# Top-k attention: the left-over values of a row are kept for each half of its chunks apart

## The reference, cut to what matters

```
q, k, v = heads(conv1x1(x, Wq, bq)), heads(conv1x1(x, Wk, bk)), heads(conv1x1(x, Wv, bv))
scores = einsum('bhnd,bhmd->bhnm', q, k) * 32 ** -0.5      # 2 x 8 x 2304 rows of 2304
kth = top_k(scores, 64)[0][..., -1:]                       # the 64th largest of each row
attn = softmax(where(scores >= kth, scores, lowest))
o = einsum('bhnm,bhmd->bhnd', attn, v)
```

## Time and profile before

| | us |
|---|---|
| median of 3 runs | 5124.61 (5120.05 to 5127.47) |
| profiled execution | 5125.56 |
| its span | 5123.8 |
| mean granted TensorE clock, share of full speed | 0.832 |

### The profile page before, as it was taken

One profiled execution on the slowest core, in us unless ns is written; L12 is line 12 of the kernel. 1 busy time (PEld: TensorE's weight loads), 2 busy tenths in 40 slices (PEclk: granted clock), 3 DMA queues, 4 the chain that ended last, 5 costly groups with the idle time before them and its releaser, 6 DMA issues. The chain is left out here.

```text
span 5123.8 us, 106951 instructions
## 1 busy us (share of the span) xinstructions
PE 4131.7 (81%) x32161; PEld 2787.5 (54%) x32161; DVE 4325.4 (84%) x25276; ACT 4155.0 (81%) x6082; POOL 1502.6 (29%) x362
## 2 busy tenths in 40 slices
PE   8577677776777677767777767899899999999999
PEld 4354444444444444544454444443567777777776
DVE  4999999999999999999999999430368888888886
ACT  2799799998999789989999899644268888888885
POOL 0344445544454444444444444200100000000000
PEclk9677777777777777777777777899799999999999
DMA  6000000000000000000000000200330111111112
GB/s 214 7 18 17 8 17 17 8 17 15 11 17 17 7 17 8 18 16 8 18 18 8 17 17 8 67 6 0 133 93 25 34 25 34 25 34 32 27 34 94
DMA packets 79597, 154.62 MB, mean 30 GB/s; under 512 B 8120, under 2 KB 49464, under 8 KB 73528
## 3 DMA queue, kind: packets, MB, share of 16 engines
q1 hardware_dynamic: 78904, 146.72, 10.1%
HBM read 99.50 MB, written 47.19 MB: 29 GB/s over the span
## 5 line engine op out<-in xcount | busy, mean ns | idle before, releaser
L542 POOL TENSOR_TENSOR a_probs<-a_scores,a_probs 128x2304 f32<-128x2304 f32 x288 | 1460.7, 5093 | 1671.3 <-ACT a_probs L465 1671.3
L560 DVE MAX8 a_top<-a_scores 128x8 f32<-128x36 f32 x18432 | 1831.6, 180 | 57.4 <-ACT a_scores L449 45.9
L376 PE MATMUL a_ps_t<-ident,a_probs 128*128 128x128 f32 x5184 | 965.2, 323 | 594.4 <-ACT a_probs_t L460 458.0
L376 PEld LDWEIGHTS a_ps_t<-ident,a_probs 128*128 128x128 f32 x5184 | 665.8, 162 | 884.4 <-ACT a_probs_t L460 597.8
L465 ACT ACTIVATE a_probs<-a_scores,a_steep_kth 128x2304 f32<-128x2304 f32 x290 | 641.2, 2211 | 183.5 <-DVE a_minus_max L692 183.5
L1292 DVE TENSOR_SCALAR_CACHE_REDUCE b_soft<-b_ps_s 128x2304 f32<-128x2304 f32 x288 | 735.0, 2552 | 26.5 <-PE b_ps_s L1151 8.5
L460 ACT ACTIVATE a_probs_t<-a_ps_t 128x512 f32<-128x512 f32 (+1 forms) x1440 | 725.8, 545 | 18.4 <-PE a_ps_t L376 6.2
L1167 PE MATMUL b_ps_t<-ident,b_soft 128*128 128x128 f32 x5184 | 727.0, 276 | 1.6 <-DVE b_soft_t L1298 0.6
L1167 PEld LDWEIGHTS b_ps_t<-ident,b_soft 128*128 128x128 f32 x5184 | 578.5, 140 | 170.3 <-ACT b_soft_t L1256 60.1
L453 ACT ACTIVATE a_probs<-a_probs,a_minus_max 128x2304 f32<-128x2304 f32 x288 | 637.9, 2215 | 30.5 <-issue 18.5
L366 PE MATMUL a_ps_s<-a_k_stack,a_q_ring 128*128 128x512 f32 (+1 forms) x1465 | 647.3, 601 | 15.9 <-ACT a_scores L449 11.1
(11 more groups left out here) (133 smaller groups left out, 4138.6 us busy)
## 6 DMA issues: line engine op xcount, KB each, us to landing
a_k_stack<-k_parts SPq DMA_DIRECT2D x72, 288.0 KB, 6.0
b_k_stack<-k_parts SPq DMA_DIRECT2D x72, 288.0 KB, 6.0
a_q_ring<-q_parts SPq DMA_DIRECT2D x294, 64.0 KB
b_q_ring<-q_parts SPq DMA_DIRECT2D x294, 64.0 KB
k_parts<-p_high SPq DMA_DIRECT2D x36, 256.0 KB, 2.1
k_parts<-p_rest SPq DMA_DIRECT2D x36, 256.0 KB, 2.1
q_parts<-p_high SPq DMA_DIRECT2D x36, 256.0 KB, 2.0
q_parts<-p_rest SPq DMA_DIRECT2D x36, 256.0 KB, 2.0
```

The lines of the kernel that those rows point to most:

```text
L376: last = pe.transpose(ps_t[(NTG * s + g) % 2][:, P * m:P * m + P], probs[s % 2][:, P * (m0 + m):P * (m0 + m) + P], cst["ident"][:, :])
L542: pool.tensor_tensor(probs[u][:, :], scores_all[:, 2 * (p % 2) + u, :], probs[u][:, :], ALU.subtract).then_inc(masked_ready, 1)
L560: last = dve.max(top8[s // 2 % 2][:, s % 2, c, :], scores_all[:, s % 4, CHUNK * c:CHUNK * c + CHUNK])
```

## The change: what it does, and the diff

`prepare` now takes the eight largest of the fourth to eighth values for chunks 0 to 31 and for chunks 32 to 63 apart: four MAX8 over 160 values for a pair instead of two over 320. The first half's eight go to column 0 of the REST rows, the second half's to column 1. The candidates are read as before, 72 x 3 a row, and hold 8 more real values. A new operation `eighths` takes the larger of the two halves' eighth values. `beyond` is formed from it and from the chunks' eighths, and stands behind `place` now. The low value is set once, before the loop, in column 2 alone.

```diff
-        extremes, beyond = sb("extremes", [P, 2, 2]), sb("beyond", [P, 2])
+        extremes, eighths, beyond = sb("extremes", [P, 2, 2]), sb("eighths", [P, 2]), sb("beyond", [P, 2])
...
+            def rest_of_half(tops, u, half):
+                return dve.max(tops[:, u, CHUNKS:CHUNKS + REST, half],
+                               tops[:, u, CHUNKS // 2 * half:CHUNKS // 2 * (half + 1), KEEP:8])
+
             def prepare(pair, tops):
 
                 wait_alone(dve, tops_taken, 2 * pair + 1)
-                counted(dve.max(tops[:, 0, CHUNKS:CHUNKS + REST, 0], tops[:, 0, 0:CHUNKS, KEEP:8]))
+                counted(rest_of_half(tops, 0, 0))
+                counted(rest_of_half(tops, 0, 1))
                 wait_alone(dve, tops_taken, 2 * pair + 2)
-                counted(dve.max(tops[:, 1, CHUNKS:CHUNKS + REST, 0], tops[:, 1, 0:CHUNKS, KEEP:8]))
+                counted(rest_of_half(tops, 1, 0))
+                counted(rest_of_half(tops, 1, 1))
...
                 after(guesses)
                 written = [0, 0]
+                counted(dve.tensor_tensor(eighths[:, :], tops[:, :, CHUNKS + REST - 1, 0],
+                                          tops[:, :, CHUNKS + REST - 1, 1], ALU.max))
                 for u in range(2):
                     rows = counted(dve.tensor_scalar(below_of(u), candidates(u), guess[:, u:u + 1], None, ALU.is_ge,
                                                      ALU.add, accum_out=above_guess[:, u:u + 1]))
-                counted(dve.tensor_tensor(beyond[:, :], extremes[:, :, 1], tops[:, :, CHUNKS + REST - 1, 0], ALU.max))
                 after(rows)
...
                 counted(dve.tensor_scalar(place[:, :], above_guess[:, :], -1.0, TOPK - 1.0, ALU.mult, ALU.add))
+                counted(dve.tensor_tensor(beyond[:, :], extremes[:, :, 1], eighths[:, :], ALU.max))
...
-                dve.memset(top8[n][:, :, CHUNKS:CHUNKS + REST, 1:KEEP], LOWEST)
+                dve.memset(top8[n][:, :, CHUNKS:CHUNKS + REST, 2:KEEP], LOWEST)
```

## The result

| | before | after |
|---|---|---|
| median, us | 5124.6 | 5076.1 (5075.2 to 5080.4) |
| ratio, with its 95% interval | | 0.9908 (0.9894 to 0.9921) |
| profiled span, us | 5123.8 | 5073.4 |
| recounts of a tile / corrections | 19 / 2 | 13 / 2 |

What follows compares the result with a forecast made beforehand. A ring through ScalarE was taken to set the period, with VectorE having a little room and searches paid in full. 5125.6 - 47 for searches + 3.5 for uncovered work gave 5082, against the median 5081 us; range 5057 to 5117.

Steps and rivals of the forecast that it cites:

- Who sets the period: Top-k hand-over: the ring runs through ScalarE, whose copy of the count sets the threshold; an ordinary pair takes 20.52 us.
- the 0.87 us of the earlier trace: Hand-over: when VectorE is late, the threshold (L691) was said to follow ScalarE's copy (L470) after 0.87 us.
- Prepare, +0.12 us: Ahead of the next scores: four maxima over 160 cost 0.91 against 0.79 us, hidden in 0.25 us of room.
- the 23 us "by it": Alternative by the Trainium skill: all added durations count, 0.05 + 0.11 us a pair beyond the room, sum about 5101.
- Select, +0.15 us, with 0.20 of room: Ahead of the doubts: eighths and the moved beyond add 0.07 us each, together 0.15, hidden in the ordinary pair.
- Rival 1: The hand-over isn't hidden: added work shows in some 130 to 144 pairs, 5088 to 5101 us; chance 0.13.
- What a search costs: Top-k stage: nothing else gets done while VectorE searches, so each is paid in full, 6.96 us plain, 14.30 corrected.
- How many go: Rows in doubt fall from 13.5 to 9.4: 4.7 plain recounts and one of two corrections go, together -47 us.
- cause B: Doubt because the left-overs' eighth value reaches the 64th: 1.45 in 10000 rows, 0.22 with the halves apart.
- cause A: Doubt because the largest of the chunks' eighth values reaches the 64th: 2.4 in 10000 rows.
- Cost without cover, +3.5 us: 14 pairs with 0.08 us of room pay 1 us, 8 without room 2.2; with the last pair +3.5.
- Rival 3: Slower: three more instructions a pair shift VectorE's jumps, each stop 1.5 us, 29 more eat the gain; chance 0.07.

Runs made afterwards that it cites:

- e5: The changed kernel with four spare two-column tensor_scalar operations between the guess and the count, ahead of the doubts: 5112.5 us, 0.9977 of before.
- e12: The kernel before with one spare two-column tensor_scalar behind the eleventh chunk maximum of the second tile: 5334.7 us, 1.0407.
- e9: The changed kernel with 64 one-column memsets ahead of VectorE's loops, which shifts the code: 5076.9 us, 0.9910 of before.
- e10: The kernel before with 64 one-column memsets ahead of VectorE's loops, which shifts the code: 5122.0 us, 0.9996.
- e1: The kernel before with no row ever in doubt, so without its 19 recounts and 2 corrections: 4981.3 us, 0.9717.
- e2: The changed kernel with no row ever in doubt, so without searches: 4978.6 us, 0.9711 of before.
- e11: The kernel before with beyond behind place, a spare two-column tensor_scalar in select and two spare MAX8 behind the extremes, all recounts kept: 5120.4 us, 0.9989.
- e4: The changed kernel with a strict comparison, so a value equal to the 64th raises no doubt: 5080.8 us, 0.9910 of before.
- e3: The kernel before with beyond behind place and three spare two-column tensor_tensor, one in select and two behind the extremes, all recounts kept: 5171.3 us, 1.0086.
- e7: The kernel before with beyond behind place and three spare two-column operations of one source (tensor_scalar), one in select, two behind the extremes: 5169.9 us, 1.0085.
- e6: The changed kernel with four spare two-column tensor_scalar operations behind the extremes, ahead of the next scores: 5151.0 us, 1.0049 of before.
- e8: The changed kernel with eighths moved from select to prepare, behind the extremes: 5104.7 us, 0.9960 of before.

## Why the prediction was right

- *Who sets the period.* Right. The added work took room and no time, the place of ScalarE's copy behind its scores stayed at 1.98 us, and e5 shows the end of that room at the step where it was said to be. In e12 the threshold stays 1.17 us behind the copy though VectorE is late. One reading in this part was wrong: the 0.87 us of the earlier trace rows was put down to VectorE being late, and it goes with the place of the pair in its head (e9, e10, e12). No term of the sum used it.
- *Prepare, +0.12 us.* Right: four maxima in 0.91 us, the idle time behind them 0.12 down. They start 0.23 us apart at a duration of 0.32, so they aren't paid at their durations. Nor does the Trainium skill say so for every case: the section that the prediction draws on, VectorE: DVE Perf Modes, The DRAIN you can't avoid, adds that a next operation that is not held starts earlier, so the 23 us "by it" go further than the page.
- *Select, +0.15 us, with 0.20 of room.* Right: 0.74 to 0.60 us from doubts to copy, so +0.14, and 0.06 is left. Rival 1 didn't come. But the pairs with no room left (0.54 us) have become 33 of 144, from 8. (The pairs like the earlier trace rows were 10 before, and not 14; their cost was put at 1 us.)
- *What a search costs.* 6.96 us plain was forecast, 7.1 came out (e1, e2), and 41.8 / 6 = 6.97 in the six periods that lost their recount.
- *How many go.* 13 recounts were forecast and 13 came. Of the corrections one of two was to go and none did. The term was -47 us and is -42.5: the 30% held, the split between plain and corrected didn't. That it held so well is partly luck, by the spread of 2.4 tiles that was given. What went must be cause B, since the change leaves cause A's comparison as it is; the shares of A and B in the count weren't measured. The formula printed for cause A is that of exactly eight values in a chunk and gives 2.2 in 10000; 2.4, and the sums made from it, are right for eight or more. Two ends of ranges are mis-added: 5124.6 - 70 + 3.5 is 5058 and not 5057, and two fewer searches give 5114 and not 5111.
- *Cost without cover, +3.5 us.* It came, and was outweighed. e1 and e2 have no searches to hide it: of their 143 periods 4 and 23 lie between 20.65 and 21.1 us, 0.9 and 5.3 us above 20.54 in sum, so 4.4 us. Yet the stage of e2 is 4.9 us shorter than that of e1, and e11's, with all searches in, 4.8 shorter than before. Six periods of e1 over 21.1 us, besides the first of a head, are gone in e2 (6.1 us; five of them at place 7 of a head), 24 instead of 16 are under 20.4 (2.4 us), and the first ones of a head give 1.2. Rival 3's mechanism, jumps that land elsewhere, is the nearest to that, and it works in both directions: maxima waiting for "issue" 10.8 us became 1.7, here in the waits of the changed kernel over the same stretch:

```profile
DVE a_steep_kth L699 <- issue: 57.9, 123, 1.8
...
DVE a_top L560 <- issue: 1.7, 8, 0.2
```

(L591, the first step of the guess, now waits 2.5 us for "issue" in 8 places, where it did not before.) A mere shift moves the stage by 4.0 us in e10, about the same size, and two like stages differ by 1.9 (e4). So 5 us of the 47 are put down to where code lies rather than to the work. That is likely and not shown: which jump gives how much stays open, and it is 0.1%.

## What to carry to other kernels

A rare branch that all engines wait for is worth its full length times its count: count how often it is taken and why, and an instruction or two in the idle time of every round can buy a good part of it. Before adding to a busy engine find out whose event ends its idle time, and measure the room to that event, section by section; a delay that passes through two sections has the room of both (e12), one in the second has only that of the second (e5). And where a small operation goes can matter more than how much it computes: eighths is free in select, 28 us in prepare, and a like one amid the maxima was 210. Which operation it is matters as well: MAX8 in the place of the held tensor_scalar cost nothing (e11).

## What was not expected of the hardware

VectorE's tensor_scalar and tensor_tensor over two columns, which take 0.16 us when GpSimd is idle, last until GpSimd's tensor_tensor over 2304 columns ends: 761 ns in the mean in e3, 771 in e7, 648 in e6, 647 in e8, 2092 in e12. VectorE's MAX8 and tensor_reduce next to them are not held up (e11, and 98 ns a maximum throughout). Where a two-column one is the first behind the reduction or amid the maxima, it ends within 0.05 us of the end of one of GpSimd's subtractions in 143 of 144 pairs (e3, e7, e8, e12; 141 in e6). What divides the held from the others here is which operation it is, and not the number of its sources in memory: tensor_scalar and MAX8 both have one. The change was free also because its only new operation of the held kind, eighths, stands in select, 13.5 us behind the threshold, where GpSimd is idle; the profile before shows that (GpSimd at work from 2.6 to 12.7 us behind each threshold), and the prediction didn't look.

The Trainium skill, SBUF — State Buffer, SBUF: two separate sides, has VectorE and GpSimd share a pair of ports that one of them holds for its whole instruction, and VectorE's operations with two sources in memory or in a mode with two ports need it. By that rule e7's tensor_scalar is a candidate as much as e3's tensor_tensor, if it runs in such a mode, which no trace here tells; the ends shown for e7, e8 and e12, 0.03 us behind GpSimd's, agree with it.
